# The product of wq and wk of a decoder layer in three f16 passes, with its split inside self-attention

## The reference

```python
x = layernorm(x + self_attention(x))          # 4 groups of 4 batches in the kernel
Q = einsum('btx,dx->btd', x, Wq) + bq         # Wq, Wk: 1024 x 1024
K = einsum('bpx,dx->bpd', ctx, Wk) + bk
scores = einsum('btd,bpd->btp', Q, K) / sqrt(1024)
x = layernorm(x + softmax(scores) @ ctx)
x = layernorm(x + ffn(x))                     # 4-bit weights
```

## Time and profile before

| | us |
|---|---|
| median of three runs | 1820.59 |
| lowest and highest | 1817.97, 1821.37 |
| the profiled execution's own time | 1816.36 |
| its span | 1814.6 |
| busy in the span: PE | 1729.8 |
| DVE | 1106.1 |
| POOL | 500.2 |
| ACT | 494.1 |

### The profile page before, as it was taken

How to read it: one execution, slowest core, us unless ns; L and a number is a source line. 1 busy time by engine, 2 the same in 40 slices (tenths; PEclk the granted TensorE clock), 3 DMA queues, 4 the chain that set the end, 5 groups by cost and what they waited for, 6 DMA issues and landing times.

```text
span 1814.6 us, 26677 instructions
## 1 busy us (share of the span) xinstructions
PE 1729.8 (95%) x9784; PEld 976.8 (54%) x9784; DVE 1106.1 (61%) x1656; ACT 494.1 (27%) x734; POOL 500.2 (28%) x326
## 2 busy tenths in 40 slices
PE   5999999898999989999999999999999899999998
PEld 3677644686878744444444444444445344444443
DVE  7787578676888877666777777877874111111111
ACT  3323110544655543322233232332332000000000
POOL 0333388133333326542232232232231000000000
PEclk8999999999999999999999999999999999999999
DMA  9353433899999967762213223223124812222120
GB/s 327 108 155 119 148 119 86 166 218 243 239 231 248 233 139 182 176 130 67 70 48 90 55 48 97 49 51 94 49 60 124 321 55 109 82 81 108 54 108 23
DMA packets 335590, 231.89 MB, mean 128 GB/s; under 512 B 288224, under 2 KB 302624, under 8 KB 333348
## 3 DMA queue, kind: packets, MB, share of 16 engines
q1 hardware_dynamic: 329284, 227.85, 48.1%
q10 hardware_dynamic: 6240, 3.15, 0.6%
HBM read 122.93 MB, written 60.83 MB: 101 GB/s over the span
## 4 chain that ended last, share of the span: by engine, by line
PE 53%; issue 25%; DVE 10%; SPq 5%; DMA 4%; ACT 1%; POOL 1%; DVEq 0%; POOLq 0%; ACTq 0%
PE psum L1671 51%; SPq L2201 4%; DMA arena<-arena 3%; DVE arena L814 1%; DVE arena L490 1%; PE psum L1922 1%; PE psum L1848 1%; DVE arena L1024 1%; DVE arena L1022 1%; DVE arena L1019 1%; PE psum L1684 1%; DVE arena L879 1%; DMA arena<-in_L_attn_Wqkv 1%; DVE arena L997 1%; POOL small L1180 1%
## 5 line engine op out<-in xcount | busy, mean ns | idle before, releaser
L1671 PE MATMUL psum<-arena 128*128 128x448 f16 (+6 forms) x7176 | 1266.9, 337 | 34.5 <-DMA arena<-arena 21.9
L1671 PEld LDWEIGHTS psum<-arena 128*128 128x128 f16 (+3 forms) x7176 | 750.3, 108 | 531.6 <-issue 85.5
L2025 PE MATMUL psum<-arena 128*128 128x512 f16 x1820 | 393.5, 379 | 6.0 <-DMA arena<-down_weights_scratch 3.7
L2025 PEld LDWEIGHTS psum<-arena 128*128 128x128 f16 x1820 | 177.7, 98 | 221.8 <-DMA arena<-down_weights_scratch 5.4
L1263 POOL TENSOR_TENSOR arena<-arena 128x1024 f16<-128x1024 f32 (+1 forms) x60 | 149.8, 2508 | 415.9 <-ACT arena L1474 415.9
L1162 DVE SCALAR_TENSOR_TENSOR arena<-psum,small,arena 128x512 f32<-128x512 f32 x28 | 20.9, 751 | 331.5 <-PE psum L2025 331.5
L1180 POOL TENSOR_TENSOR small<-small 112x1 f32<-112x1 f32 (+1 forms) x46 | 50.0, 1087 | 489.4 <-DVE small L471 489.4
L1565 ACT ACTIVATE arena<-arena,small 128x448 f32<-128x448 f32 x68 | 45.5, 668 | 207.5 <-DVE arena L1094 144.0
L1474 ACT ACTIVATE arena<-arena 128x1024 f16<-128x1024 f32 (+1 forms) x60 | 68.8, 1173 | 117.9 <-DVE arena L856 89.6
L1254 POOL TENSOR_TENSOR arena<-arena 128x224 f16<-128x224 f32 x64 | 54.3, 848 | 122.1 <-ACT arena L1445 122.0
L854 DVE TENSOR_TENSOR arena<-arena,psum 128x1024 f32<-128x1024 uint32 x65 | 79.1, 1218 | 3.0 <-PE psum L1848 0.9
(11 more groups left out here) (214 smaller groups left out, 1244.6 us busy)
## 6 DMA issues: line engine op xcount, KB each, us to landing
h_scratch<-arena SPq DMA_DIRECT2D x84, 224.0 KB, 2.9
arena<-h_scratch SPq DMA_DIRECT2D x13, 1376.0 KB, 6.1
arena<-in_ctx SPq DMA_DIRECT2D x32, 512.0 KB, 5.1
arena<-in_x SPq DMA_DIRECT2D x32, 448.0 KB, 5.7
x_scratch<-arena SPq DMA_DIRECT2D x32, 448.0 KB, 3.6
arena<-x_scratch SPq DMA_DIRECT2D x32, 448.0 KB, 4.6
arena<-in_L_ffn_down_qweight SPq DMA_DIRECT2D x21, 512.0 KB
down_weights_scratch<-arena SPq DMA_DIRECT2D x20, 512.0 KB, 3.8
```

What stands on the lines that cost most here:

```text
L1671: mm = pe.matmul(out, a, r, start=(k == 0), stop=(k == len(pairs) - 1))
L2025: mm = pe.matmul(bk[2 * s + c], ht[s][:, i, a, :], weights_of(i, w, c), start=(i == 0 and (w, a) == PASSES[0]), stop=(i == NI - 1 and (w, ...
```

## The change

The product of wq and wk is made in f16 in three passes. For this both are scaled by a power of two that depends on their largest sum of sizes over a row, and split.

- **Sizes.** In groups 1 and 2 ACT makes a pass over each chunk of wk and wq (`size`: absolute values with their sum). wq is loaded once for this, by ACT, two chunks at a time, and once more for the product. In group 3 DVE takes the largest of the sums, POOL makes one more all-reduce, and DVE the factors (`weight_factors`).
- **wk** is split within group 3: `wk_hi` on ACT (scaling in place, then cast), `wk_lo` on POOL. The f16 parts overwrite the f32 chunks from the top.
- **wq** is split chunk by chunk (`wq_hi` on ACT, `wq_lo` on POOL), the first two in group 3, the others in the loop.
- **bq*wk** and bq*bk move on POOL from the loop into groups 1 and 2, ahead of the scaling. **Wq*bk** of the first two chunks moves into group 3 (`wq_bk`). Their sums are undone with `iq` when u is copied.
- ACT's first two `m_chunk` now stand between the high parts of x1 of the last four batches, and copy M with the factor `im`.

```diff
@@ the largest and the factors, on DVE @@
+            def weight_factors():
+                dve.wait_ge(s_wb, WB0 + 2 * KC)
+                for m in range(2):
+                    w_step(dve.tensor_reduce(wbm[:, m:m + 1], wsum[:, m * KC:(m + 1) * KC], AX.X, ALU.max))
...
+                w_step(dve.tensor_scalar(im, pwb2[:, 0:1], iq, 2.0 ** -14, ALU.mult, ALU.mult))
-            self_attention(NG - 1, False)
+            self_attention(NG - 1, False, (weight_factors,))
@@ POOL @@
+            def bq_wk(lo, hi):
+                for c in range(lo, hi):
+                    pool.tensor_tensor(part, wk[:, c, :], bqc[:, c:c + 1].to_broadcast([P, D]), ALU.mult).then_inc(s_pu, 1)
+                    pool.wait_ge(s_pu, 2 * c + 1)
+                    pool.tensor_tensor(acc_v, acc_v, part, ALU.add).then_inc(s_pu, 1)
...
+            def wk_lo(c):
+                pool.wait_ge(s_wkh, KH0 + KC - c)
+                pool.tensor_tensor(wkp[:, c, 1, :], wk[:, c, :], wkp[:, c, 0, :], ALU.subtract).then_inc(s_wkl, 1)
...
             def self_attention(g, more, largest=True):
                 if more and largest:
                     x_largest(g + 1)
+                if known(g, 3) and g > 0:
+                    bq_wk((g - 1) * KC // 2, g * KC // 2)
                 for b in range(GB):
...
                     inverse_std(g * GB + b, S)
+                    if not more and 1 <= b < GB - 1:
+                        wq_bk(b - 1, b - 1)
+                    if not more and b == GB - 2:
+                        wq_lo(2, 0)
...
+            self_attention(1, True, False)
+            self_attention(2, True)
+            pool.wait_ge(s_wf1, T["wbm"])
+            pool.partition_all_reduce(wbr, wbm, P, RMAX).then_inc(s_wb, 1)
+            for c in reversed(range(KC)):
+                wk_lo(c)
+            for i in range(2):
+                wq_lo(i, i)
+            self_attention(NG - 1, False)
@@ ACT @@
+            def wk_hi(c):
+                act.activation(wk[:, c, :], wk[:, c, :], ACT.Identity, scale=fwb[:, 0:1]).then_inc(s_wks, 1)
+                if c < KC - 2:
+                    act.wait_ge(s_wkl, KL0 + KC - 2 - c)
+                act.wait_ge(s_wks, KS0 + KC - c)
+                act.activation(wkp[:, c, 0, :], wk[:, c, :], ACT.Identity).then_inc(s_wkh, 1)
...
+                    if not more and f == 2:
+                        act.wait_ge(s_wf1, T["fwb"])
+                        act.wait_ge(s_pu, 2 * KC)
+                    if not more and f >= 2:
+                        for k in range(2):
+                            wk_hi(KC - 1 - 2 * (f - 2) - k)
...
-                for b in range(GB - 2 if more else GB - 1):
+                for b in range(GB - 2 if more else GB):
                     x1_hi(g * GB + b, b, 2 * g + b // 2 + 1)
+                    if not more and b % 2 == 0:
+                        m_chunk(0, b // 2, True)
@@ PE @@
-            pe.wait_ge(s_wk, 48)
+            pe.wait_ge(s_wkl, KL0 + KC)
             def m_chunk(e, i):
-                pe.wait_ge(s_wq[i], 16 * (e + 1))
+                pe.wait_ge(s_wql, QL0 + 2 * e + i + 1)
                 pe.wait_ge(s_me, 2 * e + i + 1)
                 for h in range(2):
-                    mm = product(bk[2 * i + h], [(wq[i][:, c, :], wk[:, c, h * HALF:(h + 1) * HALF])
-                                                 for c in range(KC)])
+                    mm = product(bk[2 * i + h], [(wqx[i][:, w, c, :], wkp[:, c, a, h * HALF:(h + 1) * HALF])
+                                                 for c in range(KC) for w, a in PASSES])
```

More of the change, by code:

```diff
@@ L1383, in x1_hi, with load_wq, size @@
                 act.activation(x1p[0:S, b % 2, 0, :], yo[0:S, b % 2, :], ACT.Identity, scale=XS).then_inc(s_x1h, 1)
+            wq_v = t_in["L0_xattn_Wq"].rearrange("(p c) x -> p c x", c=KC)
+            def load_wq(m, i):
+                act.dma_start(wq[i], wq_v[:, :, bass.ds(m * P, P)]).then_inc(s_wq[i], 16)
+            sizes = [0]
+            def size(of, k):
+                if sizes[0] > 1:
+                    act.wait_ge(s_wb, WB0 + sizes[0] - 1)
+                act.activation(unread[:, sizes[0] % 2, :], of, ACT.Abs, accum_out=wsum[:, k:k + 1]).then_inc(s_wb, 1)
+                sizes[0] += 1
@@ new lines, in sizes_of_wk, with sizes_of_wq @@
+            def sizes_of_wk(lo, hi):
+                act.wait_ge(s_wk, 48)
+                for c in range(lo, hi):
+                    size(wk[:, c, :], c)
+            def sizes_of_wq(m):
+                for i in range(2):
+                    act.wait_ge(s_wq[i], 8 * m + 16)
+                    size(wq[i].rearrange("p c x -> p (c x)"), KC + m + i)
+                for i in range(2):
+                    act.wait_ge(s_wb, WB0 + sizes[0] - 1 + i)
+                    load_wq((m + 2 + i) % KC, i)
@@ new lines, in m_chunk @@
+            def m_chunk(e, i, more):
+                m = 2 * e + i
+                if more:
+                    act.wait_ge(s_uc, 4 * m + 1)
+                    act.wait_ge(s_wql, QL0 + m + 1)
+                    load_wq(m + 2, i)
+                act.wait_ge(s_m, m + 1)
+                act.activation(m32[:, bass.ds(m, 1), :].rearrange("p a b -> p (a b)"),
+                               psum[:, i * 1024:(i + 1) * 1024], ACT.Identity, scale=im).then_inc(s_me, 1)
+                if more:
+                    wq_hi(m + 2, i, KC // 2 + e + 2)
@@ L1400, in self_attention @@
                                    bias=nm1[0:S, b:b + 1], accum_out=rs1[0:S, b:b + 1]).then_inc(s_exp, 1)
+                if more and g:
+                    sizes_of_wk((g - 1) * KC // 2, g * KC // 2)
+                if not more:
+                    for c in reversed(range(1, KC // 2)):
+                        wk_hi(c)
                 if more:
@@ L1408, in self_attention @@
                     x_hi(g + 1, range(KC // 2, KC))
-                for b in range(GB - 2 if more else GB - 1):
+                if known(g, 1):
+                    act.wait_ge(s_woh, HC)
+                    act.wait_ge(s_wol, HC)
+                    for i in range(2):
+                        load_wq(i, i)
+                elif more:
+                    sizes_of_wq(4 * g - 2)
+                else:
+                    wk_hi(0)
+                    act.wait_ge(s_v, 2 * NG)
+                    for i in range(2):
+                        wq_hi(i, i, KC // 2 + 1)
+                for b in range(GB - 2 if more else GB):
                     x1_hi(g * GB + b, b, 2 * g + b // 2 + 1)
+                    if not more and b % 2 == 0:
+                        m_chunk(0, b // 2, True)
             act.wait_ge(s_xf1, 4)
@@ L1421, in _ @@
             self_attention(0, True)
-            with act.Fori(1, NG - 1) as g:
-                self_attention(g, True)
-            self_attention(NG - 1, False)
-            wq_v = t_in["L0_xattn_Wq"].rearrange("(p c) x -> p c x", c=KC)
-            def m_chunk(e, i, more):
-                act.wait_ge(s_m, 2 * e + i + 1)
-                if more:
-                    act.wait_ge(s_uc, 4 * (2 * e + i) + 1)
-                    act.dma_start(wq[i], wq_v[:, :, bass.ds((2 * e + 2 + i) * P, P)]).then_inc(s_wq[i], 16)
-                act.activation(m32[:, bass.ds(2 * e + i, 1), :].rearrange("p a b -> p (a b)"),
-                               psum[:, i * 1024:(i + 1) * 1024], ACT.Identity).then_inc(s_me, 1)
+            for g in range(1, NG):
+                self_attention(g, g + 1 < NG)
             def g_out(k, y, q):
```

90 lines of the change are left out of this document (57 added, 33 removed).

## The result

| | before | changed |
|---|---|---|
| median of four runs, us | 1820.98 | 1859.19 |
| lowest and highest | 1817.97, 1822.68 | 1856.1, 1863.01 |
| profiled execution, us | 1816.36 | 1860.7 |
| its span, us | 1814.6 | 1859.0 |

The ratio is 1.0204, with a 95% interval of 1.0182 to 1.0226: the change costs 38 us, where 40 had been forecast. The total is right. Two of the parts are not, as the trace shows.

The account below looks back on a forecast made before the run. PE, 95% busy, was taken to lean on DVE's chain of sums and layernorms without slack. 15.1 + 10.2 (groups 1, 2) + 13.5 (group 3) + 0.9 (M's stage) + 2 (clock) = 41.7 us slower: 1860, range 1838 to 1876.

Parts of the forecast that it names:

- four are 18.0: Groups 1 and 2, POOL: four chunks of bq*wk, each a multiply with its add of 4.51 us, take 18.0 us.
- 20.7 us meet 5.52 of slack: Group 1: POOL's added work ahead of the first power, less its slack, makes the first layernorm 15.1 us late.
- Group 3: From group 2's last power to M's start: all-reduce, ACT's queue and POOL's low part delay M by 13.5 us.
- layernorm 0.8, half a sum 0.7, W product of the last batch 2.6: Group 3's last step: what follows POOL's power at 229.9, so that M starts at 234.0 instead of 220.5.
- M's start to DVE's end: From the first M product to DVE's last reduction before M's factor: 114.6 us against 113.7, +0.9 (-4 to +6).
- the table work of 57.5 stays: M's stage, DVE: the table work was to take 57.5 us as before.
- rival C: Contention of POOL and DVE on the late path adds 10 us on top: 1870; chance 0.12.
- unchanged and only moved: The stages behind M's stage, cross-attention among them, were to start later but take as long as before.
- the 2 us for the clock: PE's clock drops after some five new long stops, costing 2 us (0 to 5) over the whole kernel.
- A: Rival: added POOL work hides better, changes of code shrink or overlap, half the sum goes: 1840; chance 0.12.
- B: Rival: POOL's work fits and DVE's one removable wait of 7.23 us in M's stage decides: 1813; chance 0.08.
- D: Rival: three f16 products cost no less than one f32 product in M; time as forecast, no chance of its own.

Follow-up runs that it names:

- e1: The changed kernel with the products of bq and wk left out altogether: 1830.47 us, ratio 1.0036 to the kernel before.
- e2: The kernel before with only the bq*wk products moved into groups 1 and 2, M still in f32: 1849.37 us, ratio 1.0137.
- e8: The kernel before with four small extra matmuls ahead of the logits of each cross-attention batch but the first: 1821.65 us, ratio 1.0004.
- e11: The kernel before without POOL's products of wq with bk and of bq with wk in the M loop: 1823.27 us, ratio 1.0012.
- e3: The changed kernel with the all-reduce of the weights' sizes replaced by a constant: 1851.53 us, ratio 1.0147 to the kernel before.
- e5: The changed kernel with POOL's and ACT's work at the end of group 3 reordered, nothing left out: 1852.42 us, ratio 1.0158.
- e12: The changed kernel again without any edit, on another chip: 1857.79 us, ratio 1.0204 to the kernel before.
- e4: The changed kernel with four small extra matmuls ahead of the logits of each cross-attention batch but the first: 1853.32 us, ratio 1.016.
- e7: The changed kernel with bq*wk on PE behind M, no weights' all-reduce on POOL, group 3's end reordered, and cross-attention's waits filled with matmuls: 1817.53 us, ratio 0.9966.
- e9: The four edits of e7 in another order, with bq*wk on PE ahead of M's last chunk: 1813.55 us, ratio 0.9953 to the kernel before.

## Why the prediction was right, and where it was not

**Groups 1 and 2: right in place and cause, a little small.** The steps "four are 18.0" and "20.7 us meet 5.52 of slack" hold: the products took 17.6, and e1 and e2 show from both sides that they alone do it (31 us less without them, 25 more by them). Of group 1's 18.5 us, 16.3 came at the stop itself, against 15.1 forecast and a bound of 17. One cost had been left out there: the layernorm that was waited for ran beside POOL's next add of bo and took 2.83 us instead of 0.81; this comes once in each of the three groups. The other 2.2 us lie ahead of the stop, and most of them belong to the one trace of before: from batch 0's statistics to batch 4's it has 47.4 us, where e2, e8 and e11, without ACT's passes for the sizes, have 49.1 to 49.3, and the kernels with these passes 49.0 to 50.4. So the passes cost less than 1 us, near to the nothing that the prediction gave them. In group 2 the stop cost 9.8 us, and the restart 1.6 more: the same 196 matmuls took 32.02 us instead of 30.39, at a granted clock of 0.58 in the first 4 us.

**Group 3: the right chain, 3.2 us small.** From the end of group 2's last power (218.5, worked out as 188.0) the factors came after 7.6 us (7.7 worked out), ACT's queue of high parts took 28.6 (28.8) and the power ended 41.3 after the start (41.9). The miss is in the last step, "layernorm 0.8, half a sum 0.7, W product of the last batch 2.6": the layernorm took 2.83 beside POOL's add, and the W product 4.3, at the lower clock behind the stop (0.61 granted). In e3, without both changes of code, 13.0 us of idle time on POOL, the g chunks start only 4.7 us sooner: ACT's queue is the bound, as the prediction held.

**M's start to DVE's end: the wrong step.** It is "the table work of 57.5 stays". It took 33.8, because 37 of the 57.5 us had been waits inside DVE's instructions for POOL's, and the change takes bq*wk out of the M loop: 51.5 us of POOL's work beside the table became 21.3. The rule was in the prediction, in rival C, where it was applied to the path that gets longer and not to the one that gets shorter. C's own 10 us came to some 6 on the late path, the three layernorms of 2.83. The rest of the term was 6.5 us small, not large: the last layernorm ended 24.9 us after M's start (22.4 worked out), the context came 15.2 behind it (12.6), and from the table's end to the factor were 23.5 (22.1). The low part at 282.44, which waits 9.67 us for ACT's in-order queue, had been foreseen; e5 shows that this order, with POOL's at the same place, was worth 7 us at the g chunks. In all the stage became 16.2 us shorter, where -4 had been the lower bound.

**The stages behind, "unchanged and only moved": the other wrong step.** They lost 13.3 us in the profiled execution, 9.5 of them in cross-attention (5.9 in e12) by a clock that fell after waits of 2.4 to 3.4 us; where the other 3.8 come from stays open. Instructions don't have to change for their time to do so. e4 gets 8 of them back.

The errors are -17.1 for M's stage, +11.3 for what lies behind it (the 2 us for the clock taken off), +7.9 for the three groups and +0.5 before them: +2.7 in all, rounded, from 41.7 to 44.4. Either of the first two alone would have put the time 11 or 17 us off. That they cancel was luck, and no rival described either. Of the prediction's own signs, the two that speak of M's stage failed: PE was to be idle for some 30 us behind M and DVE's table work to stay as long, and they came to 9.5 and 33.8.

**The rivals.** A (half hides) and B (only DVE's wait decides) fall with the 17.6 us measured, with the changes of code still at 5.9 to 7.1, and with e11, in which the table work is gone from the path and the time stays that of before. D is decided: a chunk takes 10.4 us.

## What to carry to other kernels

Before a span of an engine is carried over as fixed, look at what runs beside it: if the same instruction appears with 0.3 us and with 2.4, the difference is another engine's, and it moves when that engine's work moves. Work put ahead of a small instruction that another engine waits for costs its whole length less the slack, however idle its own engine is; here the same products cost 28 us on GpSimd, and 0.7 on TensorE behind M, where it had been waiting (7 in e7 and e9, where it had not). A gain in one engine's loop is worth what the second bound leaves, so find that bound first and time it without its neighbours.

## What the runs showed that was not expected

- DVE's table work is 20.6 us alone and 57.5 beside a POOL at 90%, with DVE shown as busy for 94% of it.
- POOL's change of code costs about as much on the way back as on the way out: 6.86 to 7.08 us of idle time behind an all-reduce in the changed kernel, 5.88 ahead of one. In e3 both went with the all-reduce.
- Waits of 2.4 to 3.4 us for DMAs were followed by logits of 5.71 us instead of 4.03 in half of the batches. Four matmuls of no use, about 1 us a batch, left one such batch of 14 and gained 8 us.
- A wait of 3.50 us (e3, at 514.97) and one of 2.95 (e12, at 482.67) were followed by logits at full clock, one of 2.29 (e1, at 429.86) by logits at 1.2 GHz: the wait's length alone does not decide.
